# Seven block products instead of eight for the shared up projection, with a ring of seven units

## What is computed

```python
xn = _layernorm(x)
...
gate = silu(einsum('ech,ehi->eci', xg, rg))      # 8 experts, 1024 -> 4096
up = einsum('ech,ehi->eci', xg, ru)
eout = einsum('eci,eih->ech', gate * up, rd)     # 4096 -> 1024
...
shared = silu(x @ sg) * (x @ su) @ sd            # 1024 -> 8192 -> 1024
```

## Time and profile before

| | |
|---|---|
| median of 3 runs | 3001.34 us (3000.36 to 3003.37) |
| the profiled execution | 3004.04 us, span 3002.4 us |
| PE busy | 2954.3 us, 98% of the span |
| PE weight loads busy | 2504.7 us, 83% |
| DVE busy | 1921.1 us, 64% |
| ACT busy | 1259.2 us, 42% |
| POOL busy | 66.0 us, 2% |
| DMA | 549.24 MB, mean 183 GB/s |
| mean granted TensorE clock | 0.995 of full speed |

### The profile page before, as it was taken

The page is one execution under the profiler, slowest core; times in us unless marked ns, Lnnn a source line. Parts: engine busy times, 40 slices in busy tenths (PEclk is TensorE's granted clock), DMA queues, the critical chain, the costliest instruction groups (busy, mean ns, idle before and its releaser), DMA issues.

```text
span 3002.4 us, 44063 instructions
## 1 busy us (share of the span) xinstructions
PE 2954.3 (98%) x16902; PEld 2504.7 (83%) x16902; DVE 1921.1 (64%) x2566; ACT 1259.2 (42%) x1588; POOL 66.0 (2%) x81
## 2 busy tenths in 40 slices
PE   8999999999999999999999999999999999999997
PEld 8997999878888888888888888888888888888876
DVE  8745244866666666666666666666666666666675
ACT  7622221454444444444444444444444444444451
POOL 0100000100000000000000000000000000000001
PEclk9999999999999999999999999999999999999999
DMA  3110111476666666666666666666666666666674
GB/s 107 36 57 29 57 65 43 155 250 203 209 216 207 205 209 218 209 204 210 215 207 207 207 216 208 209 209 222 210 210 211 223 210 210 211 216 210 210 240 164
DMA packets 258106, 549.24 MB, mean 183 GB/s; under 512 B 8733, under 2 KB 74525, under 8 KB 257758
## 3 DMA queue, kind: packets, MB, share of 16 engines
q1 hardware_dynamic: 253946, 532.17, 53.0%
q0 software_dynamic: 3936, 14.06, 1.5%
HBM read 537.49 MB, written 8.70 MB: 182 GB/s over the span
## 4 chain that ended last, share of the span: by engine, by line
PE 91%; DVE 4%; DMA 3%; ACT 1%; issue 1%; SPq 0%; DVEq 0%; ACTq 0%
PE ps L1589 25%; PE ps L1585 25%; PE ps L1588 25%; PE ps L1342 3%; PE ps L1398 3%; PE ps L1399 3%; PE ps L1397 3%; DVE c_lo L1180 2%; PE ps L1457 2%; DMA raw<-in_L_ffn_rd 2%; PE ps L1382 1%; DMA raw<-in_L_ffn_sd 1%; PE ps L1626 1%; DVE resid L1215 1%; PE ps L1495 1%
## 5 line engine op out<-in xcount | busy, mean ns | idle before, releaser
L1180 DVE TENSOR_TENSOR c_lo<-raw,c_hi 128x1024 fp32r<-128x1024 f32 x960 | 1126.4, 1220 | 305.7 <-ACT c_hi L674 304.5
L674 ACT CAST c_hi<-raw 128x1024 fp32r<-128x1024 f32 x960 | 953.4, 1048 | 457.8 <-DMA raw<-in_L_ffn_ru 131.6
L1585 PE MATMUL ps<-yT_hi,c_hi 128*128 128x314 f32 (+1 forms) x2048 | 628.0, 307 | 0.4 <-issue 0.4
L1588 PE MATMUL ps<-yT_lo,c_hi 128*128 128x314 f32 (+1 forms) x2048 | 628.1, 307 | 0.0
L1589 PE MATMUL ps<-yT_hi,c_lo 128*128 128x314 f32 (+1 forms) x2048 | 627.7, 307 | 0.0
L1589 PE MATMUL ps<-c_hi,xgT_lo 128*97 128x512 f32 x1024 | 403.4, 394 | 0.0
L1585 PE MATMUL ps<-c_hi,xgT_hi 128*97 128x512 f32 x1024 | 402.2, 393 | 0.0
L1588 PE MATMUL ps<-c_lo,xgT_hi 128*97 128x512 f32 x1024 | 401.3, 392 | 0.0
L1585 PEld LDWEIGHTS ps<-yT_hi,c_hi 128*128 128x128 f32 x2048 | 385.9, 188 | 2.7 <-DVE c_lo L1180 0.4
L1588 PEld LDWEIGHTS ps<-yT_lo,c_hi 128*128 128x128 f32 x2048 | 386.2, 189 | 1.8 <-issue 0.5
L1589 PEld LDWEIGHTS ps<-yT_hi,c_lo 128*128 128x128 f32 x2048 | 385.9, 188 | 0.0
(11 more groups left out here) (229 smaller groups left out, 3377.9 us busy)
## 6 DMA issues: line engine op xcount, KB each, us to landing
raw<-in_L_ffn_rg SPq DMA_DIRECT2D x128, 1024.0 KB, 5.5
raw<-in_L_ffn_ru SPq DMA_DIRECT2D x128, 1024.0 KB, 5.6
raw<-in_L_ffn_rd SPq DMA_DIRECT2D x128, 1024.0 KB, 6.2
raw<-in_L_ffn_sg SPq DMA_DIRECT2D x32, 1024.0 KB, 6.0
raw<-in_L_ffn_su SPq DMA_DIRECT2D x32, 1024.0 KB
raw<-in_L_ffn_sd SPq DMA_DIRECT2D x32, 1024.0 KB, 8.1
wl<-in_L_mix_w_qkv SPq DMA_DIRECT2D x6, 2048.0 KB, 7.7
wl<-in_L_gnn_W SPq DMA_DIRECT2D x2, 2048.0 KB, 29.4
```

The source lines that it names most:

```text
L674: nc.scalar.copy(order.view(c_hi[u % RING], u), part(raw[r % RAW])).then_inc(sem("hi_done"), 1)
L1180: V.tensor_tensor(order.view(c_lo[u % RING], u), part(raw[r % RAW]), order.view(c_hi[u % RING], u).bitcast(F32), ALU.subtract).then_inc(se ...
L1585: m = MM(out_, l_hi, r_hi, start=first, stop=False)
L1588: MM(out_, l_hi, r_lo, start=False, stop=False)
```

## The change

The shared up product is written as a product of 2 x 2 blocks and computed in seven block products (Strassen's scheme in Winograd's form) instead of eight. The weight pair [gate, up] of 1024 x (256 + 256) is cut in the middle of k and between gate and up: A11 (gate, first half of k), A21 (up, first half), A22 (up, second half), A12 (gate, second half), each one raw block of 512 KB. The tokens are cut in the middle of k and between the two halves of 314.

- **Tokens.** `yT_hi` and `yT_lo` give way to seven token blocks of 128 x 4 x 314 (B11, B21, B22, and the differences T1 to T4), each with hi and lo, made once ahead of and during the first step.
- **Weights.** Per step DVE makes four sums in place in the raw buffers (`factor_sum`), and seven factors are split: units 0 to 6 of a step. The step has 33 units (counted as U = 35), the ring has 7 slots, and the raw data lie in five buffers of 512 KB, 30 blocks a step.
- **Products.** `products(j)` for the two column blocks j: seven products of 4 k-tiles x 3 matmuls x 314 columns. ACT copies banks between products (`seed`), and later products accumulate on the copy; one result is kept in SBUF (`keep_e7`). DVE adds it to two banks (`shared_up`), multiplies by silu and splits at 628 columns at once (`shared_inner`).
- **Orders.** ACT, DVE and PE lists are arranged anew; SBUF addresses move; small buffers are merged (`r_silu`, `s_h`).

```diff
-U = 30
+RING = 7
+UNITS = 33
+U = 35
-RING = 10
-RAW = 3
-BLK = 15
+RAW = 5
+BLK = 30
...
+F_A11, F_S3, F_S2, F_A12, F_S1, F_A22, F_S4 = range(NPROD)
+FACTOR_RAW = (R_A11, R_A21, R_A21, R_A12, R_A11, R_A22, R_A12)
+SUM_BEFORE = (0, 1, 2, 0, 3, 0, 4)
+BANKS = ((X0, X0 + 1, X0 + 2, X0 + 3), (R0, R0 + 1, X0 + 2, X0 + 3))
+TO_B, TO_E7, TO_C, TO_D = 1, 2, 3, 4
...
+        last = {R_A11: F_S1, R_A22: F_A22, R_A12: F_S4, R_A21: F_S4}
...
+STEP = Order(s=0, gate=(7, 15), sd=23, rd=25, a_bank=(A0, R0))
+FIRST = Order(s=0, sd=7, gate=(9, 17), rd=25, a_bank=(A0, X0))
+LAST = Order(s=24, gate=(0, 8), sd=31, rd=16, a_bank=(A0, X0))
...
+        def factor_hi(e, q, order, i):
+            u = order.s + i
+            r = order.raw(u)
+            if SUM_BEFORE[i]:
+                act.wait_ge(sem("sums"), count(e, q, 4, SUM_BEFORE[i]))
+            else:
+                act.wait_ge(sem(f"raw_in{r % RAW}"), count(e, q, 16 * BLK // RAW, 16 * (r // RAW + 1)))
+            act.wait_ge(sem("unit_used"), count(e, q, U, u + 1 - RING + USED0))
+            nc.scalar.copy(c_hi[u % RING][:], raw[r % RAW][:]).then_inc(sem("hi_done"), 1)
...
+            def seed(j, n):
+
+                a, c, b, d = BANKS[j]
+                to = {TO_B: b, TO_C: c, TO_D: d}[n]
+                product_done(j, {TO_B: F_A11, TO_C: F_S2, TO_D: F_S1}[n])
+                nc.scalar.copy(PS[to][:, 0:HW], PS[a][:, 0:HW]).then_inc(sem("seeded"), 1)
+
+            def keep_e7(j):
+                product_done(j, F_S3)
+                act.wait_ge(sem("s_up"), count(e, q, 4, 2 * j + ONE))
+                nc.scalar.copy(e7[:], PS[BANKS[j][3]][:, 0:HW]).then_inc(sem("seeded"), 1)
...
+            def shared_seeds(j, *between):
+
+                for f, n in zip((lambda: seed(j, TO_B), lambda: keep_e7(j), lambda: seed(j, TO_C),
+                                 lambda: silu_shared(j, 0), lambda: seed(j, TO_D), lambda: silu_shared(j, 1)),
+                                between + ((),) * 6):
+                    f()
+                    for u in n:
+                        hi(u)
...
-            for u in range(10):
+            for u in range(4):
                 hi(u)
-            silu_shared(0)
-            silu_shared(1)
+            hi(4)
+            shared_seeds(0, (5,), (6,))
             if q == 0:
                 tokens_hi(0)
                 tokens_hi(1)
-            hi(10)
-            hi(11)
-            silu_shared(2)
-            silu_shared(3)
-            for u in range(12, 22):
+            shared_seeds(1, (7,), (8,), (9,), (10,), (11, 12), (13,))
+            for u in range(14, 21):
                 hi(u)
             silu_routed(0)
-            for u in range(22, 28):
+            for u in range(21, 30):
                 hi(u)
             turned_hi(0)
             silu_routed(1)
-            hi(28)
-            hi(29)
             turned_hi(1)
+            for u in range(30, 33):
+                hi(u)
...
+            if i == F_S3:
+                for r in (R_A11, R_A21):
+                    b = order.b0 + r
+                    dve.wait_ge(sem(f"raw_in{b % RAW}"), count(e, q, 16 * BLK // RAW, 16 * (b // RAW + 1)))
+                ins = V.tensor_tensor(rc, ra, rc, ALU.subtract)
+            elif i == F_S2:
+                b = order.b0 + R_A22
+                dve.wait_ge(sem(f"raw_in{b % RAW}"), count(e, q, 16 * BLK // RAW, 16 * (b // RAW + 1)))
+                dve.wait_ge(sem("lo_done"), count(e, q, U, U + order.s + F_S3 + 1))
+                ins = V.tensor_tensor(rc, rd_, rc, ALU.subtract)
+            elif i == F_S1:
+                dve.wait_ge(sem("sums"), count(e, q, 4, SUM_BEFORE[F_S2]))
+                ins = V.tensor_tensor(ra, rc, ra, ALU.add)
+            else:
+                dve.wait_ge(sem("lo_done"), count(e, q, U, U + order.s + F_A12 + 1))
+                ins = V.tensor_tensor(rb, rb, rc, ALU.subtract)
...
+            def factors():
+
+                lo(order.s + F_A11)
+                sums(F_S3)
+                lo(order.s + F_S3)
+                sums(F_S2)
+                lo(order.s + F_S2)
+                sums(F_S1)
+                lo(order.s + F_A12)
+                lo(order.s + F_S1)
+                sums(F_S4)
+                lo(order.s + F_A22)
+                lo(order.s + F_S4)
...
+            factors()
             routed_add(count(e, q, U, USED0), cleared)
+            shared_up(0)
             shared_inner(0)
...
+            for u in range(7, 12):
+                lo(u)
+            shared_up(1)
+            lo(12)
+            shared_inner(1)
+            for u in range(13, 21):
                 lo(u)
             routed_inner(0)
-            for u in range(22, 27):
+            for u in range(21, 30):
                 lo(u)
-            shared_add(0)
-            lo(27)
+            routed_inner(1)
             turned_lo(0)
...
+            for n in range(2 * NT):
                 shared_add(n)
             turned_lo(1)
+            for u in range(30, 33):
+                lo(u)
...
+            def products(j, between={}):
+
+                a, c, b, d = BANKS[j]
+                bank = (a, d, a, b, a, c, d)
+                after = {F_S2: TO_B, F_A12: TO_B, F_S1: TO_C, F_A22: TO_C, F_S4: TO_D}
+                for i in range(NPROD):
+                    u = order.s + i
+                    t = FACTOR_TOK[i]
                     split(u)
...
+                    if i == F_S3 and j == 1:
+                        pe.wait_ge(sem("silu_done"), count(e, q, 6, order.silu_s + 2))
+                    if i in after:
+                        pe.wait_ge(sem("seeded"), count(e, q, 8, 4 * j + after[i]))
+                    for k in range(4):
+                        col = slice(k * 256 + j * P, k * 256 + (j + 1) * P)
+                        m = three(PS[bank[i]][:, 0:HW], c_hi[u % RING][:, col], c_lo[u % RING][:, col],
+                                  tok_hi[t][:, k, :], tok_lo[t][:, k, :], k == 0 and i not in after, k == 3,
+                                  skip=(i in after))
+                    m.then_inc(sem("unit_used" if j else "s_half"), 1)
```

More of the change, by code:

```diff
@@ L110, in shared @@
-    def shared(self, u):
-        return self.s <= u < self.s + 4
-    def source(self, u):
-        def rows(half):
-            return lambda t: t[:, half * 1024:(half + 1) * 1024]
-        def columns(j):
-            return lambda t: t[:].rearrange("p (k n) -> p k n", k=KT)[:, :, j * P:(j + 1) * P]
+        self.b0 = self.block(s)
+        last = {R_A11: F_S1, R_A22: F_A22, R_A12: F_S4, R_A21: F_S4}
+        self.last_unit = [s + last[b - self.b0] if self.b0 <= b < self.b0 + 4 else
+                          next(u for u in range(UNITS) if not self.shared(u) and self.block(u) == b)
+                          for b in range(BLK)]
@@ L121, in source, with block, raw @@
+    def shared(self, u):
+        return self.s <= u < self.s + NPROD
+    def block(self, u):
+        return u if u <= self.s else u - (NPROD - 4)
+    def raw(self, u):
         if self.shared(u):
-            return (self.s + (u - self.s) % 2 * 2) // 2, columns((u - self.s) // 2)
-        return u // 2, rows(u % 2)
-    def view(self, t, u):
-        return t[:].rearrange("p (k n) -> p k n", k=KT) if self.shared(u) else t[:]
+            return self.b0 + FACTOR_RAW[u - self.s]
+        return self.block(u)
@@ L367, in tokens_part, with y_columns, turned_y, f32 @@
         return hi[s], lo[s], fill_bank(n)[:, 0:4 * TP].rearrange("p (k n) -> p k n", k=4)
+    TILE2 = HW - 2 * TP
+    def y_columns(t):
+        if t == 2:
+            return (slice(2 * TP, HW), slice(0, TILE2)), (slice(0, 3 * TP - HW), slice(TILE2, TP))
+        return ((slice(t * TP, (t + 1) * TP), slice(0, TP)), None) if t < 2 else \
+               (None, (slice(t * TP - HW, (t + 1) * TP - HW), slice(0, TP)))
+    YA = [sum(1 if t != 2 or h == 0 else 2 for t in range(NT) for h in range(2)
+              if 2 * t + h <= j and not (h == 0 and t > 2)) for j in range(2 * NT)]
+    YD = [sum(1 for t in (2, 3, 4) if 2 * t <= j) for j in range(2 * NT)]
+    def turned_y(j):
+        return PS[TB_Y[(YT0 + j) % 3]][:, 0:4 * TP].rearrange("p (k n) -> p k n", k=4)
+    def f32(b):
+        return tok_32[b][:]
     def weights_part(g, i):
@@ L721, in step @@
+                block_hi(T3)
+                block_hi(T2)
+                seed(0, TO_B)
+                block_hi(T1)
+                keep_e7(0)
+                hi(3)
+                block_hi(B22)
+                seed(0, TO_C)
+                hi(4)
+                block_hi(T4)
+                hi(5)
+                silu_shared(0, 0)
+                squares(2, 4)
+                seed(0, TO_D)
+                squares(4, NT)
+                hi(6)
                 logits_out(0)
-                squares(1, 2)
@@ L877, in _, with factor_sum, factor_lo @@
             count_group(gr, between[gr])
+        def factor_sum(e, q, order, i):
+            ra, rc, rd_, rb = [raw[(order.b0 + r) % RAW][:] for r in range(4)]
+            n = SUM_BEFORE[i]
```

(17 more changed lines are left out.)

493 lines of the change are left out of this document (284 added, 209 removed).

## The result

| | before | after |
|---|---|---|
| median | 3001.9 us (3000.4 to 3003.4, 4 runs) | 3154.5 us (3148.9 to 3160.2, 4 runs) |
| ratio | | 1.051, 95% interval 1.049 to 1.053 |
| span of the profiled execution | 3002.4 us | 3158.5 us |
| mean granted clock of TensorE over the span | 0.995 | 0.969 |

The change makes the kernel 5.1% slower. The forecast was 1.2%, with a range that ended at 3088. The sign was right and the size was wrong by a factor of four: 152.6 us in place of 37.

The account below looks back on a forecast made before the run. PE, busy 98% of the span, was taken as the bound. Thirty steady steps of -3.4+3.3+0.3+0.85 give +31, first step +7, last -1: 3004.0+37, less 2.7, is 3038 us; range 2975 to 3088.

Parts of the forecast that it names:

- The cause and place of the pause in the products: Before each step's third product, PE waits for a bank copy queued on ACT behind a hi awaiting DVE's sum; 3.26 us.
- the term of 3.3: Steady step, shared up products: PE's wait for the bank copy costs 3.3 us a step.
- The routed part: Routed up into shared down: late weight blocks delay the residual add; 0 to 0.8 us a step, taken as 0.3.
- The rival of the starving ring: Routed up: blocks landing after 5 us, not 3.5, starve PE, 1 to 2 us a step more; 3085 us; chance 0.08.
- The clock: Behind the products' pause: half clock for 3.4 us would cost 1.7; bounds 0 to 1.7 a step, taken as 0.85.
- the second rival: The products' pause comes but the clock holds among plain matmuls; 3013 us; chance 0.24.
- The first step: First step: DVE's token block sums and lo's make PE wait; +7 us, bounds 0 to 16.
- The last step: Last step: stall 0.3, saving 3.4, and +2 for final additions among DVE's residual adds; together -1 us.
- The seeds aren't late: Shared up products: the bank copy comes early, leaving only lo waits of 1.3 us a step; 2953 us; chance 0.14.
- the rival of slow products: Shared up products take more than 0.1443 us a matmul, 0.01 more being 1.7 us a step; 3090 us; chance 0.04.

Follow-up runs that it names:

- e1: Changed kernel with only the first bank copy of each step moved ahead of the hi conversions it stood behind in ACT's queue; 3116.8 us, ratio 1.038.
- e4: Changed kernel with twenty filler matmuls, results unused, in front of the third product of the steady steps; 3117.7 us, ratio 1.037.
- e8: Changed kernel with only the sum S3 moved ahead of the lo of A11 in DVE's queue; 3073.7 us, ratio 1.024.
- e2: Changed kernel with three of shared down's residual adds moved between the lo's of units 27, 28 and 29 in DVE's queue; 3075.5 us, ratio 1.023.
- e5: Changed kernel with three residual adds early, two bank copies ahead of hi's that wait for sums, and sum S3 ahead of the lo of A11; 2927.6 us, ratio 0.975.
- e7: Changed kernel with the early residual adds and both early bank copies of e5, but without its moved sum; 2968.6 us, ratio 0.989.
- e9: e2 plus twenty filler matmuls in the pause before the third product; 3028.7 us, ratio 1.0075.
- e10: e2 plus ten filler matmuls in the pause before the third product, leaving pauses of 1.85 us on average; 3046.8 us, ratio 1.0147.

## Why the prediction was wrong, point by point

**The cause and place of the pause in the products: right.** With 0 at the start of routed down (1591.96 in this step, next products 1603.09), ACT and PE of after:
```profile
1597.74 1.05 ACT L634 CAST c_hi<-raw 128x1024 fp32r<-128x1024 f32 x1 [2.20 <-PE ps L1803]
1601.29 1.05 ACT L634 CAST c_hi<-raw 128x1024 fp32r<-128x1024 f32 x1 [2.50 <-DVE raw L993]
1604.96 1.99 ACT L634 CAST c_hi<-raw 128x1024 fp32r<-128x1024 f32 x2 [2.62 <-DVE raw L998]
1608.51 1.04 ACT L634 CAST c_hi<-raw 128x1024 fp32r<-128x1024 f32 x1 [1.55 <-DVE raw L1001]
1609.46 0.41 ACT L770 COPY ps<-ps 128x314 f32<-128x314 f32 x1
```
```profile
1609.93 0.63 PE L1799 MATMUL ps<-tok_hi,c_hi 128*128 128x314 f32 x1 [3.21 <-ACT ps L770]
```
hi A11 at 5.78 (forecast 5.86), hi S3 9.33 (9.35), hi S2 13.00 (12.95), hi S1 16.55 (16.44), copy 17.50 (17.39), product S2 17.97 (17.88). The copy takes 0.41 (0.43 from the silu of the same shape). A chain that is worked out from a few rows of durations and handovers held within 0.11 us over 18 us. A step shows 3.1 us of idle time for it, as the term of 3.3 said (less 0.17, by which a matmul's row of 0.31 outlasts its share of 0.14). e1, e4 and e8 change this pause alone, and the row of the residual adds stays at 62 to 74 us in all three.

**The routed part: wrong, 2.1 us a step in place of 0.3.** This step of the sum carried three estimates, and the one that failed is the time to land. The trace of before has blocks of 1 MB only the earlier trace rows; half of one I took as 3.4 to 3.6 us from a single issue that ran alone. The median of these blocks of 512 KB in after is 5.3, and 5.5 for the six issued from 1565 to 1574. The working priced the transfers' rate rightly (1.49 us a block; the window below moves 342 GB/s, 1.53), but let the blocks arrive one unloaded latency behind their slot. The window of routed up's end, then ACT and DVE of after, where shared down starts at 1573.71:
```profile
1565.00:1578.00 13.00, 13.00 (x61) 9.57 (x60) 10.00 (x10) 8.77 (x9) 0.00 (x0) 1.00 0.93 342
```
```profile
1573.84 1.05 ACT L752 CAST c_hi<-raw 128x1024 fp32r<-128x1024 f32 x1 [1.86 <-DMA raw<-in_L_ffn_rd]
```
```profile
1574.92 5.01 DVE L1342 TENSOR_TENSOR c_lo<-raw,c_hi 128x1024 fp32r<-128x1024 f32 x4 [1.69 <-ACT c_hi L752]
1579.85 0.69 DVE L1364 TENSOR_TENSOR r_h<-ps,r_h 97x512 f32<-97x512 f32 x1
...
1580.92 2.47 DVE L1405 TENSOR_TENSOR resid<-ps,resid 125x512 f32<-125x512 f32 x4
```
```profile
1581.66 0.49 PE L1799 MATMUL ps<-c_hi,sh_hi 128*125 128x512 f32 x1 [2.15 <-DVE resid L1405]
```
ACT waits 1.86 us for a block; the lo of unit 29 ends at 1579.93, which is 6.2 us after routed up ends, where the forecast had 3.6 to 4.7; behind it stand the three instructions that the prediction names, and the first add ends at 7.9, not 5.6 to 6.7. The late block alone would have been harmless, as e2 shows; that PE waits is the order. The prediction saw this queue and still priced it near the lower end of its bounds. The rival of the starving ring had the landing right ("after 5 us") and the place wrong: routed up itself does not pause, its lead of seven units carries it, and the bill comes one stage later.

**The clock: wrong, 2.0 to 2.6 us a step in place of 0.85, and above the bound of 1.7.** Two parts of that step failed. It gave one half-clock stretch of 3.4 us to half of the steps. In fact the products' pause brings the clock down 30 times of 31, and the second pause, which was not in the forecast, 9 times more (table above); and a stretch lasts 4.0 us on average (163.8/41). That puts 5.1 us of half clock on a step (153.6/30). What it cost shows in PE's busy time over the thirty steps, idle time left out: 2256.4 us in after, 2178.1 in e5, for the same instructions. The difference of 78.3 us, 2.6 a step, is the most that the clock can have cost. Some of it is a small loss at each pause: e7, with 3.4 us at half clock in these steps and some 50 more short pauses than e5, is busy for 15.9 us more (2194.0), 0.3 a pause. An estimate with this taken off for the 60 more pauses of after leaves 60 us, 2.0 a step, which is two fifths of the low time, as in e9. The rows of before could not settle this; the second rival (the clock holds) fell: its ground was that pauses of 3 us among plain matmuls might be stood, and the table shows them to fall in 59 of 64 cases, and e10 behind 1.77 us.
The Trainium skill, TensorE: Matmul & The Clock Gate, section "Part 4: PE-mode transpose", was that rival's support, by its sentence that transposes do not count as PE-busy as matmuls do. The runs here neither refute nor need it: what they show is that a fall needs no transposes near it: the last ones stand ahead of routed down, over 14 us before the copy's pause.

**The first step: +7 forecast, +5.5 measured**, with PE's wait for the lo of the tokens at 6.1 us, once. **The last step: -1 forecast, +6.3 measured.** It keeps the pause of 3.2 behind the copy and has two of 1.8 and 3.1 in front of the transposes, put down to DVE's routed product (row `r_h` above). The copy there was priced at 0.3, since the first hi starts early; the copy is behind the hi of the last sum all the same.

**The sum again, with measured terms**, for a steady step: -3.3 (PE's busy time, before less e5) +3.1 (copy) +2.1 (residual add) +2.6 (the clock, and the small loss at each pause) +0.3 (waits for issue) = +4.8, as in the ledger. Of the 152.6 us, 37 were forecast; of the rest some 54 are the second pause (30 x 1.8), 53 the clock with the loss at the pauses (30 x 1.75), 7 the last step. Either of the two big ones alone would have put the time at 3091 or 3092, just past the range.

**The rivals.** "The seeds aren't late" was priced at 2953 for a kernel whose copies run early. e7 is that kernel, with the adds in order, at 2968.6. The products came at 0.1445 us a matmul (20 in 2.89 us from 1603.09 on), so the rival of slow products is out. None of the rivals reached 3154, because each varied one cost and held the rest, and the costs came together.

**What stays open.** Why the clock falls behind one pause of 1.77 us and not behind an equal one of the next step: between them only the place of the pause in time differs, and no run here separates that. Of e2's 79 us, 64 are the pause and, at two fifths of 30.7 us, some 12 the clock; the other 3 have no row of their own. Of e8's 29 us over its expectation 10 are the longer wait of the residual adds and some 13 the eight more falls of the clock behind them (two fifths of 8 x 4.0 us); the rest was not followed up.

## What to carry to other kernels

A saving on the engine that sets the time arrives only if the work added on the others stands in the right place of their queues: here the same instructions were 5.1% slower or 2.5% faster by the order of six of them in each step. For each added instruction that another engine waits for, write down what stands in front of it in its queue and when that is released, for the whole step and not up to the first stall found, since a stall hides the next one. Price a smaller transfer at the latency that its queue shows under load, and price a pause of 2 to 3 us of TensorE at more than its length: here 5.2 us of such pauses a step brought 2.0 to 2.6 us more in slower matmuls behind them.
